# One planning cost in an attention order: VectorE's last maximum of a unit, 0.15 to 1.9

## The reference, cut to what matters

```
x   : (8, 1024, 512)      cond: (8, 1024)
x   = x + attention(x, cond)     # 16 heads of 32, modulated q, k, v, w, u weights
x   = x + scan_block(x, cond)    # projection, conv, silu, layernorm, state scan, gate, projection

attention (per batch b, head h):
  q, k = heads(norm(x * s1) @ Wq.T * qdc), heads(norm(x * s1) @ Wk.T * kdc)
  p    = softmax(q k^T / sqrt(32));  out = p v
```

## Time and profile before

| | us |
|---|---|
| median of 3 runs (6010.3 to 6031.31) | 6021.95 |
| profiled execution, device time | 6045.26 |
| its span | 6043.3 |
| TensorE busy in the span | 5770.7 (95%) |
| VectorE busy | 4388.4 (73%) |
| GpSimd busy | 3185.9 (53%) |
| ScalarE busy | 2411.4 (40%) |
| granted clock, mean | 0.979 |

### The profile page before, as it was taken

How to read it: one execution, slowest core, us unless ns; L and a number is a source line. 1 busy time by engine, 2 the same in 40 slices (tenths; PEclk the granted TensorE clock), 3 DMA queues, 4 the chain that set the end, 5 groups by cost and what they waited for, 6 DMA issues and landing times.

```text
span 6043.3 us, 74674 instructions
## 1 busy us (share of the span) xinstructions
PE 5770.7 (95%) x24986; PEld 2610.9 (43%) x24986; DVE 4388.4 (73%) x5652; ACT 2411.4 (40%) x4726; POOL 3185.9 (53%) x2561
## 2 busy tenths in 40 slices
PE   7999999999999999999989999999999999999999
PEld 3444444444444444444435434434344444434334
DVE  4656556565565656656534899999999999999994
ACT  2444444444444444444445333434243433434110
POOL 1777667776676767666664142434434242434313
PEclk7999999999999999999999999999999999999999
DMA  2332323323233232322322444444445344444543
GB/s 88 84 99 64 100 60 112 96 66 102 60 109 95 63 102 62 114 82 58 99 70 105 107 123 107 125 133 122 137 113 151 99 143 110 133 126 124 140 116 122
DMA packets 415984, 622.82 MB, mean 103 GB/s; under 512 B 59088, under 2 KB 192336, under 8 KB 415088
## 3 DMA queue, kind: packets, MB, share of 16 engines
q1 hardware_dynamic: 378736, 567.68, 33.2%
q10 hardware_dynamic: 36864, 50.38, 3.3%
HBM read 310.56 MB, written 205.57 MB: 85 GB/s over the span
## 4 chain that ended last, share of the span: by engine, by line
PE 70%; DVE 18%; issue 4%; ACT 2%; ACTq 2%; POOL 2%; DMA 1%; DVEq 1%; SPq 0%; POOLq 0%
DVE g L2223 9%; PE bank L820 8%; PE bank L850 8%; PE bank L808 6%; PE miscb L1979 5%; PE misc L837 5%; PE yps L1940 5%; DVE g L2229 5%; PE bank L779 3%; PE bank L761 3%; PE miscb L1871 3%; PE bank L789 3%; PE yps L1871 3%; PE xps L1926 2%; PE miscb L1950 2%
## 5 line engine op out<-in xcount | busy, mean ns | idle before, releaser
L1161 POOL TENSOR_TENSOR acc<-acc,prob 128x512 f32<-128x512 f32 x1536 | 1908.1, 1279 | 853.9 <-PE bank L850 571.7
L1090 DVE TENSOR_REDUCE mx<-bank 128x1 f32<-128x512 f32 x2048 | 1308.2, 686 | 542.7 <-PE bank L820 536.5
L2223 DVE SCALAR_TENSOR_TENSOR g<-xps,bd,g 128x1024 f32<-128x1024 f32 x1024 | 1313.1, 1282 | 118.9 <-PE xps L1926 89.6
L983 ACT ACTIVATE prob<-misc 128x512 f32<-128x512 f32 x1277 | 713.5, 598 | 760.7 <-PE misc L837 675.1
L820 PE MATMUL bank<-khat,qhat 96*128 96x512 f32 x2048 | 940.5, 520 | 20.5 <-DVE xt_s L1067 15.3
L2229 DVE TENSOR_SCALAR g<-g,lim 128x1024 f32<-128x1024 f32 x1024 | 832.1, 813 | 34.6
L837 PE MATMUL misc<-qhat,khat 98*128 98x512 f32 x1443 | 602.6, 460 | 18.2 <-ACT prob L983 12.4
L820 PEld LDWEIGHTS bank<-khat,qhat 96*128 96x128 f32 x2048 | 374.0, 192 | 548.7 <-issue 383.1
L1940 PE MATMUL yps<-g,cexp 128*32 128x512 f32 x4096 | 499.8, 606 | 0.0
L808 PE MATMUL bank<-xhT,wqk 128*128 128x512 f32 x1024 | 490.2, 605 | 2.6 <-ACT rsum L989 1.7
L850 PE MATMUL bank<-prob,V 128*32 128x512 f32 x3584 | 488.9, 615 | 0.2 <-ACT prob L983 0.2
(11 more groups left out here) (246 smaller groups left out, 7752.3 us busy)
## 6 DMA issues: line engine op xcount, KB each, us to landing
sx<-scratch_xhl SPq DMA_DIRECT2D x512, 128.0 KB, 5.3
scratch_dx<-dx SPq DMA_DIRECT2D x64, 512.0 KB, 2.8
scratch_xhl<-xhi SPq DMA_DIRECT2D x64, 512.0 KB, 4.0
scratch_xhl<-xn SPq DMA_DIRECT2D x64, 512.0 KB, 4.7
scratch_y<-ysb SPq DMA_DIRECT2D x512, 64.0 KB
early<-scratch_dx SPq DMA_DIRECT2D x59, 512.0 KB, 4.7
early<-scratch_y SPq DMA_DIRECT2D x59, 512.0 KB, 3.6
xt_n<-in_x SPq DMA_DIRECT2D x112, 256.0 KB, 3.0
```

Of the source, the lines that this page charges most:

```text
L983: act.activation(to, bank[m][:, 0:QC], ACT.Exp, scale=SCALE).then_inc(sem[f"act_m{m}"], 1)
L1090: dve.tensor_reduce(self.mx2[:, h * TT + qt, c:c + 1], bank[m][:, 0:QC], AX.X, ALU.max).then_inc(sem[f"dve_m{m}"], 1)
L1161: pool.tensor_tensor(self.acc[:, a, h, :], self.acc[:, a, h, :], self.prob[:, (n % 2) * GH + h, :], ALU.add).then_inc(sem["pool_acc"], 1)
L2223: dve.scalar_tensor_tensor(self.g[:, t % STATES, :], self.xps[t % 2][:, :], self.bd[:, i % 2, tl:tl + 1], self.g[:, (t - 1) % STATES, :], ...
```

## The change

The planning cost of the piece "mxr" goes from 0.15 to 1.9. No instruction, semaphore rule or data layout is edited; the order of `plan.pieces` of the attention is made anew with this cost, and with it the banks that pieces get.

```diff
@@ def maxima(u)
-        put("DVE", 0.15, ("mxr", u), (("mr", u, GH * n_steps - 1),) + ((("mt", u - 1),) if u else ()), [("dve_mx", 1)])
+        put("DVE", 1.9, ("mxr", u), (("mr", u, GH * n_steps - 1),) + ((("mt", u - 1),) if u else ()), [("dve_mx", 1)])
         g = ("mt", u)
         put("PE", 0.2, g, (("mxr", u),), [("pe_m{m}", 1)], take=SIDE, group=g)
         put("ACT", 0.3, ("mh", u), (g,) + ((("mst", u - 1),) if u else ()), [("act_mh", 1)])
```

## The result

The changed kernel takes 5982.61 us (median of 4 runs, 5979.32 to 5989.14) against 6025.63 for the kernel before (4 runs): a ratio of 0.9936, 95% interval 0.9920 to 0.9953, 28 to 48 us less. The prediction was 5989 with a range of 5966 to 6018. Five more runs, in another session, gave 5980.99 against 6022.31, ratio 0.9931 (0.9918 to 0.9943). One later execution, of the kernel in e7, ran at a granted clock of 0.584 and took 13759.62 us; it is left out of that kernel's median and ratio.

A forecast was written before the change was run, and what follows sets the result against it. TensorE was taken to bound the attention; gains at the transpose of 7.0 + 5.1 + 9.1 + 10.3 + 1.4 = 32.9 us, taken from the median 6021.95, gave 5989 us, range 5966 to 6018.

The forecast's parts named there:

- What bounds: Attention, 150 to 3175 us: TensorE is the bound, busy 2912.6 of 3025 us; an order can win its idle 112.
- Why mxr is late: VectorE's queue before mxr: 32 wait instructions at 0.097 us each, 2.28 us idle per unit, cost more than result waits.
- The term of mt: TensorE's transpose waiting for mxr: work moved ahead wins 32.9 of 41.0 us, leaving about 8.
- kind 3: Units 3, 7, ... 27: one piece of 1.00 us goes ahead of mt; gain 7 x 1.00 = 7.0 us.
- unit 31: Last attention unit: S already waits 1.20 us for the maxima's DMA, so filling mt's idle 1.13 gains 0.
- kind 5: Units 5, 9, ... 29: two pieces, together 1.3 us, go ahead of mt; gain 7 x 1.3 = 9.1 us.
- Swap of work, priced at 0 with bounds of +-6 us: Ahead of S in seven units: one or two ready projection pieces change places, priced at 0, bounds +-6 us.
- L1047: VectorE instruction taking 8.58 us in two of seven places, costing TensorE 15.3 us; kept unchanged in the sum.
- a sign that the prediction named as speaking against it: TensorE's waits: the forecast is wrong if L1067 appears there with another count than two.
- Rival 1: The two long L1047 go away: 32.9 + 15.3 = 48 us gained, 5974; chance 0.10.
- What is late next: Behind mt: S waits for mrow only in unit 31, about 1.2 us; elsewhere the shortest distance, 5.7, exceeds 4.20.
- How long L1047 is held: VectorE beside GpSimd's adds: the skill's rule implies waiting one add; measured 8.58 us outlasts several, so trace disagrees.

The follow-up runs named there:

- e7: Changed kernel's order with the loop of 64 waits run backwards, so few waits remain; 5981.92 us, ratio 0.9943 against the kernel before.
- e1: Kernel before with mxr's cost left at 0.15 but its result counted as landed 1.75 later, delaying only the transpose; 5985.38 us, ratio 0.9937.
- e3: Kernel before, same order, with the loop waiting for 64 maxima run backwards, 4 waits instead of 64; 5980.47 us, ratio 0.9930.
- e6: Planning cost of mxr set to 2.5 instead of the change's 1.9; 5970.97 us, ratio 0.9930 against the kernel before.
- e8: Kernel before, unchanged, executed once more for a second profile; span 6011.0 us against 6043.3 in the first.
- e9: Changed kernel, unedited, run and profiled again in a later session; 5980.99 us, ratio 0.9931 against the kernel before.
- e4: Kernel before with L1047's product of two SBUF tiles replaced by a reduction over one SBUF input; 6018.89 us, ratio 0.9996.

## Why the prediction was right, step by step

**What bounds.** Right. TensorE's wait at L827 was what the order could win. The runs e1, e3 and e6, three different ways to remove it, end at 5971 to 5985, and with two of them together (e7) it is no better.

**Why mxr is late.** Right, by e3: 32 wait instructions of 0.097 us.

**The term of mt.** The sum said 32.9 of 41.0 us; 39.9 went (41.0 to 1.1). The term was 7 us too small, by the assumption that the order stays and single pieces move ahead of mt. 4.5 of the 7 are in kind 3, where the gain was capped at 1.00 per unit by one C; in fact the whole tail was placed anew, with the last maxima earlier in TensorE's list, and the idle time there is 0.0 in all units of that kind. 1.1 are unit 31, put at 0, where mt's idle time went and S's wait for mrow hardly changed. Only u = 17, 21, 25 and 29 keep 0.2 to 0.3 us, in kind 5, and not kind 3, where most of the 8 us were to stay.

**Swap of work, priced at 0 with bounds of +-6 us.** Mis-sized, and on the losing side: the new order costs TensorE 11 to 13 us in spacing. It isn't the swap in front of S that does it but more long spacings behind L837, over the whole unit.

**L1047.** Kept in the sum as they were, and this is where a sign that the prediction named as speaking against it came true: L1067 appears in the waits not with two of 7.65 us but with one of 0.2. It did no harm to the number, since no timed execution of before shows the two long ones and no profile of the changed kernel has one; that is luck. But then the profiled 6043.3 us hold what the median does not: the 15.3 us and a lower clock, which the prediction saw only as "23.3 us above the median". It could have been read from that: a stall of 2 x 7.65 us in a profile whose time lies above all runs (6031.31 the highest) is likely the profile's own. Rival 1 (5974) was no event of the order.

**What is late next.** Right: mrow's wait stays one of 1.1 us in unit 31 (1.8 in the second profile, against 1.2 and 1.5 before). The shortest distance from mt to S elsewhere is 6.98 us (unit 15), since C did not move ahead of mt. Where it did, with mt alone later (e1), the shortest is 5.56 us, near the 5.7 of the prediction, and S doesn't wait there either. L837's waits for ScalarE did not take up what mt gave either: 26.0 us in all against 30.1 in the first profile of before, 23.5 against 26.2 in the second ones.

**The sum of the attention**, between the second profiles (e8 and e9): idle 83.4 - 39.2 = 44.2 us less, of which 40.3 at L827; half clock (53.5 - 51.3) / 2 = 1.1 less; spacing 3032.1 - 3020.7 = 11.4 more. That is 33.9 against 3130.8 - 3097.0 = 33.8 measured. At equal clock the timed runs gain 5902.1 - 5870.2 = 31.9 us. The forecast of 32.9 met this by two errors of opposite sign, 7 us too little at mt and some 12 us for spacing that were put at 0, and by the idle time elsewhere that fell too; the mechanism was right, the closeness is luck. The medians say 43.0 and, in the later session, 41.3, interval 34 to 49; the 9 us above 31.9 there are the clock, 0.9816 in the mean against 0.9801. The clock has no term in the prediction.

**How long L1047 is held.** By the Trainium skill (page "SBUF — State Buffer", section "Summary: rules for kernel authors") the second of two such instructions waits until the first finishes. In e8 the trace agrees: each L1047 ends with the one add that was running (0.86 and 1.24 us). The 8.58 us in the first profile don't: there VectorE was held through seven operations of GpSimd.

## What to carry to other kernels

When a small instruction on a fast engine has a long idle time called "issue" before it, count the wait instructions in its queue: a loop of waits for values that grow on one semaphore costs about 0.1 us each, and only the last value is needed. Run the loop backwards, or give the planner the cost that the profile shows; either removes the stall of the bound engine, and both together bring nothing more. Before a stall of one profile goes into a sum, see whether the profiled time lies within the timed ones, or profile again. And set the clock apart before small gains are compared: time x mean granted clock told 7 us between two kernels whose medians agree.

## What the runs showed of the hardware

- A standalone semaphore wait whose value is already there takes VectorE's queue 0.097 us (32 in 3.0 us), more than the 0.04 us between dependent instructions with two waits (0.69 us of work, next start at 0.73).
- A VectorE instruction with two SBUF inputs of 8 columns took 0.17 to 1.25 us beside GpSimd's adds and ended with the add that was running, or took 8.58 us and ended when GpSimd next stood idle; 1.24 and 8.58 came from the same place of the same program in two executions. With one SBUF input it took 0.16 us in all seven places (e4).
- TensorE's score matmuls start 0.338 us apart when two of L820 follow each other, and 0.236 us apart when an L837 follows an L820 (medians).
- The granted clock is a cost like a wait: the same instructions behind the attention took 2870.3 us with 82 us at 0.5 and 2897.1 us with 130 us at 0.5, and 2690 to 2695 us in all 12 profiles once idle time and half of that time are taken off.
